# A two-layer transformer block on one core: projection in pieces within the attention plan, spectral fold at its end

## The chip, the cores and the metric

The kernel runs on one NeuronCore of one Trainium2 chip. The metric is the time of one execution in microseconds on the device, lower is better. The engines are named as in the profile: PE (TensorE, matmuls), PEld (its weight loads), DVE (VectorE), ACT (ScalarE), POOL (GpSimd) and SP (SyncE, which here issues nearly all DMAs).

## What is computed

```python
def proj(w):                                    # L0 attention: 16 heads of 16, 2 batches x 2048 tokens x 256
    return (x @ w).reshape(b, l, N_HEADS, HEAD_DIM).transpose(0, 2, 1, 3)
q, k, v = (proj(q_w), proj(k_w), proj(v_w))
scores = jnp.einsum('bhid,bhjd->bhij', q, k) / scale + alibi[None]
scores = jnp.where(causal[None, None], scores, -jnp.inf)
out = jnp.einsum('bhij,bhjd->bhid', softmax(scores), v) ... @ o_w
...
y = jnp.real(ifft(einsum('bnd,do->bno', fft(x), w)))     # L0 feed-forward: spectral, linear in x
...
x = _layernorm(x + _L0_attn_ref(...)); x = _layernorm(x + _L0_ffn_ref(...))
x = _layernorm(x + _L1_attn_ref(...)); x = _layernorm(x + _L1_ffn_ref(...))
```

The second layer (a channel attention and eight experts) is not touched by the change.

## The kernel before

The program has a front part, which computes the first attention up to its division by the softmax sums, and a back part with all the rest. Each engine walks the same list of steps (`front_plan`, then a back plan) and issues its own instructions of each step, so the list fixes the order on every engine.

**Projection.** The 4096 tokens are 8 tiles of 512; tiles 0 to 3 are batch 0. For each tile `TurnX` transposes x (L803), four `Project` steps (L820, 128x512 in f32) give two halves of q and of k, and two `Values` steps (L834) give v. ACT takes a projected half from PSUM as bf16 (L1213, the high part), DVE forms the rest (L1377), ACT its bf16 (L1216, the middle part), POOL what is left (L1749, the low part), and SP stores the three parts to `split_dram` (L1826) from one of four buffers `parts`. ACT waits for the store that last used a buffer (`parts_out`) before it writes that buffer again.

**Attention.** A unit is one batch and four of its sixteen heads: 8 units, u0 to u7. SP loads a unit's operands from `split_dram` in one of three places: 4 loads of constant key rows (L1873), one of query rows (L1878), 24 of 64 KB (L1888) and 6 of 256 KB (L1886), 35 DMAs in all. A first pass (`Chunk`, L875 with the masks of L881) computes scores into a ring of two PSUM slots of two banks, and DVE takes their row maxima (L1398). After each quarter of a unit (`Maxima`, qt 0 to 3) POOL splits the maxima, PE turns them (`SendMaxima`, L889), DVE copies them (L1414), and SP writes them as three more operand rows (L1839, `max_t`). Only then may the second pass of that quarter begin: `Score` (L909, three PSUM banks), `exp` on ACT (L1231), `Select` on POOL for the diagonal blocks (L1769), `Weigh` (L927: probabilities times v). `TakeSums` and `Divide` (L938) end a quarter. `Attention` orders these by estimated times for each engine.

**Order before.** Four tiles are projected, then come `Operands(0)`, `FoldSpectral` (L847, L854: three 256x256 products that fold the spectral weights into one matrix) and `Operands(1)`. Tiles 4 to 7 then alternate with chunks of u0, `PULL_A` columns for each piece; `Operands(2)` follows, and then the first `Score`. Projection has PSUM banks of its own (2, 3, 7, and 0 and 1 for the transposes). `x_t` holds all of x transposed.

Of the kernel before, what the change touches and what calls it, by code (L numbers as in the profile page):

```python
# [43 lines left out]
PULL_A = 1536  # L44
# [12 lines left out]
AT_A, AT_SPEC = 2 * OPS, OPS  # L57
# [5 lines left out]
PROJECT_BANKS = (2, 3, 7)  # L63
# [7 lines left out]
TurnX = namedtuple("TurnX", "tile half")  # L71
Project = namedtuple("Project", "tile side m n bank rested copied slot")
Values = namedtuple("Values", "tile half n bank rested copied")
FoldSpectral = namedtuple("FoldSpectral", "")
Operands = namedtuple("Operands", "u scored first count")
LOADS = 1 + len(TERMS) * (1 + QT)
PadRow = namedtuple("PadRow", "")
ClearSums = namedtuple("ClearSums", "")
Chunk = namedtuple("Chunk", "u qt r heads c width per_bank ring slot before")
Maxima = namedtuple("Maxima", "u qt t ring turned_before")  # L80
SendMaxima = namedtuple("SendMaxima", "u qt t ring slot before")
# [4 lines left out]
Divide = namedtuple("Divide", "u qt t ring slot before")  # L86
Residuals = namedtuple("Residuals", "ring")


class FrontPlan:  # L90


    def __init__(self):
        self.steps = []
        self.n_bank = self.n_split = self.n_values = 0
        self.bank_rested, self.bank_copied = {}, {}
        self.ring_slots, self.ring_at, self.ring_of = [0, 1], 0, {}

    def ring(self):
        n, slot = self.ring_at, self.ring_slots[self.ring_at % len(self.ring_slots)]  # L100
        before = self.ring_of.get(slot, -1) + 1
        self.ring_of[slot] = n
        self.ring_at += 1
        return n, slot, before

    def bank(self, rests):
        b = PROJECT_BANKS[self.n_bank % (2 if self.ring_at else 3)]
        self.n_bank += 1
        rested, copied = self.bank_rested.pop(b, 0), self.bank_copied.pop(b, 0)
        if rests:  # L110
            self.bank_rested[b] = self.n_split + 1
        else:
            self.bank_copied[b] = self.n_values + 1
        return b, rested, copied

    def project_tile(self, tile):
        self.steps += [TurnX(tile, 0), TurnX(tile, 1)]
        for side in range(2):
# [39 lines left out]

STRIPE = 32
UNIT_COLUMNS = GH * LENGTH * (LENGTH + P) // 2 // P  # L160


class Attention:

# [161 lines left out]
    def step(self):  # L326
# [21 lines left out]
        if self.act < self.pe + 1400:  # L348
            order.append("score")
# [1744 lines left out]
```

## Time and profile before

| | us |
|---|---|
| median of 3 runs (lowest, highest) | 1605.79 (1602.51, 1612.28) |
| profiled execution | 1608.99 |
| span of its trace | 1607.2 |
| PE, DVE, ACT, POOL busy in it | 1425.7, 1069.6, 862.0, 240.7 |

The profiled execution took 1.8 us more than the span of its trace and 3.2 us more than the median. Busy time of PE counts an instruction from start to its modelled end, so overlapping matmuls hide gaps that their starting times show.

### The profile page before, as it was taken

What the parts mean: (1) busy time and instruction counts of PE and PEld (TensorE: products, weight loads), DVE (VectorE), ACT (ScalarE), POOL (GpSimd) and SP (SyncE); (2) the same over time, 40 slices, a digit from 0 to 9 for tenths busy, and PEclk for the clock granted to TensorE, in tenths of its full rate; (3) what the DMA queues carried; (4) which work ended last, traced back from release to release, by engine and by line L of the source; (5) the groups of instructions that cost most, each with busy time, mean ns of one, the idle gap of its engine ahead of it and who ended that gap; (6) DMA issues with size and microseconds to landing.
All of it is one profiled execution on the core that took longest, in us unless ns stands there. A gap on an engine that the chain in (4) does not pass through costs nothing. (4 is left out here: it accounts for less than half of the span.)

```text
span 1607.2 us, 43807 instructions
## 1 busy us (share of the span) xinstructions
PE 1425.7 (89%) x18356; PEld 856.1 (53%) x18356; DVE 1069.6 (67%) x1985; ACT 862.0 (54%) x1791; POOL 240.7 (15%) x380
## 2 busy tenths in 40 slices
PE   7657749999989999999999999899877639999998
PEld 4433314444444444444444443487754329999997
DVE  2135538888888878888888884165357736776776
ACT  3212336776767767767677677664325513333333
POOL 4212201111110111002110120000012531111111
PEclk9979969999999999999999999899798859999999
DMA  7794550131322412315120000282004154545451
GB/s 239 147 125 116 117 52 3 27 45 21 52 28 35 62 21 37 42 30 68 20 48 3 3 4 2 77 297 64 1 0 160 57 195 161 190 168 189 169 191 71
DMA packets 76383, 134.08 MB, mean 83 GB/s; under 512 B 11938, under 2 KB 62619, under 8 KB 70812
## 3 DMA queue, kind: packets, MB, share of 16 engines
q1 hardware_dynamic: 69612, 120.14, 31.0%
q0 software_dynamic: 3408, 8.43, 1.5%
q8 instruction: 146, 2.39, 0.7%
q10 hardware_dynamic: 3168, 2.72, 0.6%
q14 instruction: 49, 0.40, 0.1%
HBM read 67.77 MB, written 23.11 MB: 57 GB/s over the span
## 5 line engine op out<-in xcount | busy, mean ns | idle before, releaser
L1398 DVE TENSOR_REDUCE part_max<-pair 128x2 f32<-128x1024 f32 (+2 forms) x576 | 645.0, 1162 | 144.8 <-PE pair L881 85.1
L1231 ACT ACTIVATE big<-pair 128x512 f32<-128x512 f32 (+1 forms) x1120 | 566.7, 613 | 233.0 <-PE pair L909 230.6
L875 PE MATMUL pair<-big 128*32 128x512 bf16 (+3 forms) x5120 | 357.4, 350 | 39.5 <-DMA big<-split_dram 24.9
L909 PE MATMUL pair<-big 128*32 128x512 bf16 (+3 forms) x5120 | 354.9, 352 | 36.3 <-DMA big<-max_t 34.1
L927 PE MATMUL pair<-big 128*17 128x512 f32 (+3 forms) x2560 | 281.8, 529 | 12.6 <-POOL big L1769 7.9
L875 PEld LDWEIGHTS pair<-big 128*32 128x32 bf16 x5120 | 136.0, 97 | 201.3 <-DVE part_max L1398 71.4
L909 PEld LDWEIGHTS pair<-big 128*32 128x32 bf16 x5120 | 126.4, 96 | 208.8 <-ACT big L1231 104.6
L1244 ACT ACTIVATE std<-moments,eps_col 128x1 f32<-128x1 f32 (+1 forms) x110 | 32.5, 295 | 258.4 <-DVE moments L1441 258.4
L1769 POOL TENSOR_SCALAR_AFFINE_SELECT big<-big 128x512 f32<-128x512 f32 x128 | 80.0, 635 | 513.7 <-ACT big L1231 513.7
L1145 PE MATMUL pair<-big,tok 128*128 128x128 f32 x1248 | 147.7, 277 | 2.7 <-DMA tok<-big 1.5
L1145 PEld LDWEIGHTS pair<-big,tok 128*128 128x128 f32 x1248 | 147.2, 194 | 5.2 <-DVE big L1669 3.3
L1157 PE MATMUL pair<-big 128*128 x624 | 141.0, 379 | 0.0
L1157 PEld LDWEIGHTS pair<-big 128*128 128x128 f32 x624 | 115.6, 190 | 14.1
L927 PEld LDWEIGHTS pair<-big 128*17 128x17 f32 x2560 | 68.5, 96 | 75.9 <-issue 35.6
L881 PE MATMUL pair<-masks,ident_b 128*32 128x128 bf16 x2048 | 101.5, 221 | 0.0
L1806 POOL DMA_INDIRECT out<-big x39 | 38.4, 984 | 262.6 <-DVE big L1710 262.6
L820 PE MATMUL pair<-big 128*128 128x512 f32 x128 | 65.1, 649 | 8.5 <-issue 5.2
L881 PEld LDWEIGHTS pair<-masks,ident_b 128*32 128x32 bf16 x2048 | 56.5, 98 | 25.3 <-issue 18.3
L983 PE MATMUL pair<-big 128*128 128x256 f32 x256 | 58.5, 382 | 0.0
L1377 DVE SCALAR_TENSOR_TENSOR big<-pair,big 128x512 f32<-128x512 f32 x32 | 22.1, 691 | 53.8 <-ACT big L1213 53.7
L1749 POOL TENSOR_TENSOR big<-big 128x512 bf16<-128x512 f32 x32 | 37.0, 1156 | 128.9 <-ACT big L1216 128.9
L1340 ACT ACTIVATE big<-pair,columns 128x128 f32<-128x128 f32 x156 | 44.2, 365 | 20.4 <-PE pair L1145 13.9
(162 smaller groups left out, 1273.1 us busy)
## 6 DMA issues: line engine op xcount, KB each, us to landing
tok<-big SPq DMA_DIRECT2D x39, 1024.0 KB
big<-in_L_ffn_w SPq DMA_DIRECT2D x16, 1024.0 KB, 12.1
split_dram<-big SPq DMA_DIRECT2D x32, 384.0 KB, 2.7
big<-split_dram SPq DMA_DIRECT2D x192, 64.0 KB, 6.3
big<-split_dram SPq DMA_DIRECT2D x48, 256.0 KB, 7.8
big<-routed_dram SPq DMA_DIRECT2D x39, 129.0 KB, 2.1
tok<-in_L_attn_x SPq DMA_DIRECT2D x8, 512.0 KB, 11.5
big<-in_c_query_rows SPq DMA_DIRECT2D x8, 512.0 KB, 5.3
```

The costliest lines, as they stand in the source:

```text
L820: mm = pe.matmul(m.bank[step.bank], m.w_qkv0[step.side][:, c, step.m * P:(step.m + 1) * P], m.x_t[:, c, cols], start=(c == 0), stop=(c == ...
L875: mm = pe.matmul(bank[q:q + STRIPE, o:o + w], m.q_op[slot][:, step.qt, h, step.r * P + q:step.r * P + q + STRIPE], m.k_op[slot][:, h, step ...
L881: mm = pe.matmul(bank[q:q + STRIPE, o + w - P:o + w], m.ident_b[:, q:q + STRIPE], m.masks[:, 1, :], start=False, stop=True, skip_group_che ...
L909: mm = pe.matmul(m.bank[step.bank][k:k + STRIPE, n * w:(n + 1) * w], m.k_op[slot][:, h, step.kb * P + k:step.kb * P + k + STRIPE], m.q_op[ ...
L927: mm = pe.matmul(m.sums[32 * h:32 * h + HD + 1, q0:TILE], m.v_aug[:, b * BPB + kb, g * GH + h, :], m.p_ring[:, place, h, at:at + TILE - q0 ...
L983: mm = pe.matmul(m.bank[b][:, j * D:(j + 1) * D], m.turned_x[slot][:, c, r * P:(r + 1) * P], weight[:, c, :], start=(c == 0), stop=(c == K ...
L1145: mm = pe.matmul(m.bank[b][:, j * P:(j + 1) * P], w1[:, c, f * P:(f + 1) * P], m.xln_t[i % 2][:, c, :], start=(c == 0), stop=(c == KC - 1))
L1157: mm = pe.matmul(m.bank[b][:, 0:D], m.hidden_t[i % 2][:, f, :], m.w2[:, bass.ds(e, 1), f, :].rearrange("p a n -> p (a n)"), start=(f == 0) ...
L1231: act.activation(m.p_ring[:, step.place, step.heads[0]:step.heads[-1] + 1, step.at:step.at + w], m.bank[step.bank][:, 0:len(step.heads) * ...
L1340: done = act.activation(m.hidden_t[i % 2][:, j, :], m.bank[b][:, j * P:(j + 1) * P], ACTF.Relu, bias=col[:, j, bass.ds(e, 1)])
L1398: dve.tensor_reduce(m.part_max[(step.u * QT + step.qt) % 2][:, step.r, step.heads[0]:step.heads[0] + n, step.c], banks[:, :, 0:w], X, ALU. ...
L1769: pool.affine_select(weights, weights, pattern=[[0, GH], [1, P]], compare_op=ALU.is_ge, fill=zero, base=0, channel_multiplier=-1).then_inc ...
```

## The change

The projection becomes 32 pieces: for each tile the transposes, a pair (q and k of one half), the values, and the other pair. Each piece takes a slot of the first pass's ring (`take_room`), so banks 0 to 2 belong to the second pass from the beginning. One planner orders all: tiles 0 to 3 are due at once, the pieces of tiles 4 to 7 when the second pass has done set shares of a unit. ACT's two copies of a projected half are separate steps, `High` and `Middle`. There are three `parts` buffers instead of four. For u0 operands are loaded tile by tile (`FirstOperands`: 12 loads of 64 KB when a tile's first pair is stored), the constant rows of u0 ahead of them. The copies of v are shared by ACT and DVE. The spectral fold and its five loads stand behind the last unit's first pass, in the ring. The planner's constants change a little (LAG 70 to 80, PE_LAG 170 to 190, ROWS_LAG 2500 to 3000, and the costs of some steps), and two blocks are weighed together only when both are ready.

```diff
-PULL_A = 1536
+PARTS = 3
...
+def project_pieces():
+    for tile in range(TILES):
+        yield "turn", tile, 0
+        yield "project", tile, 0
+        yield "values", tile, 0
+        yield "project", tile, 1
...
+    def project_due(self):
+        late = self.n_project - 4 * TPB
+        return late < 0 or self.score_columns > UNIT_COLUMNS * (0.1 + late / (4 * TPB))
 
...
-        unit = self.chunks[self.n_chunk][0]
-        now = self.scores[min(self.n_score, len(self.scores) - 1)][0]
-        done = self.score_columns / len(UNITS)
-        if self.n_score and (unit > now + 1 or self.max_columns > self.score_columns + self.lead()):
+        u, qt = self.chunks[self.n_chunk][:2]
+        at = self.operands_at.get((u, qt))
+        lead = UNIT_COLUMNS * (1 - 0.5 * self.score_columns / (len(UNITS) * UNIT_COLUMNS))
+        if at is None or self.max_columns > self.score_columns + lead:
             return None
-        return self.ring_at()
...
+    def project(self):
+        kind, tile, m = self.projects[self.n_project]
+        self.n_project += 1
+        if kind == "turn":
+            room = self.take_room("turn", tile)
+            self.steps.append(TurnX(tile, room))
+            self.pe += 900
+            self.act = max(self.act, self.pe + self.PE_LAG) + 500
+            self.dve = max(self.dve, self.pe + self.PE_LAG) + 620
+            self.free[room.slot] = self.turned_at[tile] = max(self.act, self.dve) + self.LAG
+        elif kind == "values":
+            room = self.take_room("values", tile)
+            self.steps.append(Values(tile, room))
+            self.pe += 3450
+            self.act = max(self.act, self.pe + self.PE_LAG) + 500
+            self.dve = max(self.dve, self.pe + self.PE_LAG) + 620
+            self.free[room.slot] = self.valued_at[tile] = max(self.act, self.dve) + self.LAG
+        else:
+            room = self.take_room("pair", self.n_pair)
+            self.steps.append(Project(tile, m, self.n_pair, room))
+            for side in range(2):
+                n = 2 * self.n_pair + side
+                self.pe += 1720
+                self.flush_middles(False)
+                self.steps.append(High(tile, side, m, n, n % PARTS))
+                self.act = max(self.act, self.pe + self.PE_LAG) + 500
+                self.dve = max(self.dve, self.act + self.LAG) + 620
+                self.middles.append((Middle(tile, side, m, n, n % PARTS), self.dve + self.LAG))
+            self.free[room.slot] = self.dve + self.LAG
+            self.n_pair += 1
+    def flush_middles(self, force):
+        while self.middles and (force or self.middles[0][1] <= self.act):
+            step, at = self.middles.pop(0)
+            self.steps.append(step)
+            self.act = max(self.act, at) + 520
+            self.pool = max(self.pool, self.act + self.LAG) + 1160
+            if step.side == 1:
+                self.stored(step)
+    def stored(self, step):
+        at = self.pool + 12000
+        if step.tile < TPB and step.m == 0:
+            self.steps.append(FirstOperands(step.tile, step.n))
+            self.operands_at[0, step.tile] = at
+        if (step.tile, step.m) == (TPB - 1, 0):
+            self.steps.append(Operands(1, 0, step.n, 0, LOADS))
+            for qt in range(QT):
+                self.operands_at[1, qt] = at + 28000
+        if (step.tile, step.m) == (TILES - 1, 1):
+            self.steps.append(Operands(2, 0, step.n, 0, LOADS))
+            for qt in range(QT):
+                self.operands_at[2, qt] = at + 28000
 
...
+    def fold(self):
+        n, room = self.take_ring()
+        if self.folds.pop(0) == "first":
+            self.fold_ring = n
+            self.steps.append(FoldFirst(n, room))
+            self.pe += 7100
+            self.dve = max(self.dve, self.pe + self.PE_LAG) + 1250
+        else:
+            self.steps.append(FoldSecond(n, self.fold_ring, room))
+            self.pe += 3600
+            self.dve = max(self.dve, self.pe + self.PE_LAG) + 1100
+        self.free[room.slot] = self.fold_at = self.dve + self.LAG
...
 def front_plan():
     plan = FrontPlan()
-    steps = plan.steps
-    for tile in range(TPB):
-        take(plan.project_tile(tile), 6)
-    steps += [Operands(0, 0, 0, LOADS), FoldSpectral(), Operands(1, 0, 0, LOADS)]
-    attention = Attention(plan)
-    owed = 0
-    attention.chunk()
-    for tile in range(TPB, TILES):
-        for _ in plan.project_tile(tile):
-            owed += PULL_A
-            while attention.max_columns < min(owed, UNIT_COLUMNS):
-                if attention.to_send and attention.to_send[0][-1] <= attention.pe:
-                    attention.send()
-                attention.chunk()
-    steps += [PadRow(), Operands(2, 0, 0, LOADS), ClearSums()]
-    while attention.step():
+    while plan.step():
         pass
-    plan.divided_ring = attention.divided_ring
+    plan.ring_at = plan.n_ring
+    assert not plan.loads and not plan.folds and plan.n_project == len(plan.projects)
     return plan
 
 
...
+def wait_room(pe, s, room):
+    if room.taken:
+        pe.wait_ge(s.ring_taken, room.taken)
+    if room.turned:
+        pe.wait_ge(s.xt_by_act, room.turned)
+        pe.wait_ge(s.xt_by_dve, room.turned)
+    if room.rested:
+        pe.wait_ge(s.rested, room.rested)
+    if room.valued:
+        pe.wait_ge(s.v_by_act, room.valued)
+        pe.wait_ge(s.v_by_dve, room.valued)
...
+        elif isinstance(step, Project):
+            pe.wait_ge(s.xt_by_act, step.tile + 1)
+            pe.wait_ge(s.xt_by_dve, step.tile + 1)
+            wait_room(pe, s, step.room)
+            for side, b in enumerate(MAX_BANKS[step.room.slot]):
+                if step.pair == 0:
+                    pe.wait_ge(s.w0_in[side], 16)
                 for c in range(KC):
...
+            if step.n >= PARTS:
+                act.wait_ge(s.parts_out[step.slot], 16 * (step.n // PARTS))
+            act.activation(m.parts[step.slot][:, 0, :], pair_bank(m, plan, step.n), ACTF.Copy,
                            scale=float(scale)).then_inc(s.high, 1)
+        elif isinstance(step, Middle):
             act.wait_ge(s.rested, step.n + 1)
             act.activation(m.parts[step.slot][:, 1, :], m.rest[step.slot][:, :], ACTF.Copy).then_inc(s.middle, 1)
 
...
+                 t["c_query_rows"].bitcast(BF16)[:, 0, :, :, :]).then_inc(s.first_in[0], 16)
     for step in plan.steps:
-        if isinstance(step, Project):
+        if isinstance(step, Middle):
             sp.wait_ge(s.low, step.n + 1)
             sp.dma_start(m.split_dram[step.side, :, step.m * P:(step.m + 1) * P, step.tile * TILE:(step.tile + 1) * TILE]
                          .rearrange("a p n -> p a n"), m.parts[step.slot][:, :, :]).then_inc(s.parts_out[step.slot], 16)
...
+            if step.n == 0:
+                sp.wait_ge(s.pool_set, 2)
+                sp.dma_start(m.routed_dram[EXPERTS * REGION:, :], m.pad_row).then_inc(s.pad_row_out, 16)
+        elif isinstance(step, FirstOperands):
+            first_operands(sp, m, s, step)
 
         elif isinstance(step, Operands):
             load_operands(sp, m, s, step)
+        elif isinstance(step, FoldLoads):
+            sp.wait_ge(s.scored, step.scored)
+            for dst, src in (("cos", "c_cos"), ("sin", "c_sin"), ("nsin", "c_nsin"), ("wr", "L0_ffn_w_freq_real"),
+                             ("wi", "L0_ffn_w_freq_imag")):
...
+def wait_parts(sp, s, n):
+    for slot in range(PARTS):
+        stored = (n - slot) // PARTS + 1
+        if stored > 0:
+            sp.wait_ge(s.parts_out[slot], 16 * stored)
...
+def first_operands(sp, m, s, step):
+    wait_parts(sp, s, step.stored)
+    cols = slice(step.tile * TILE, (step.tile + 1) * TILE)
+    for i in range(len(TERMS)):
+        rows = slice(EXTRA + i * HD, EXTRA + (i + 1) * HD)
+        sp.dma_start(m.k_op[0][rows, :, cols], operand_source(m, 0, i, 1, cols)).then_inc(s.first_in[step.tile], 16)
+        sp.dma_start(m.q_op[0][rows, step.tile, :, :], operand_source(m, 0, i, 0, cols)).then_inc(s.first_in[step.tile], 16)
...
-                for i in range(4):
```

In the order of instructions this shows at three places. (`pair0` to `pair3` are PSUM banks 0-1, 2-3, 4-5, 6-7; an instruction's first shape is what its rows multiply.)

SP, from the last loads of `Operands(1)` (L1888, L1886) to the first maxima rows (L1839). Before, with L1826 a store of parts:

```order
L1888 DMA big<-split_dram 16x4x512 x4
L1886 DMA big<-split_dram 16x4x2048
L1826 DMA split_dram<-big 128x3x512 x8
L1839 DMA big<-max_t0 1x16x128 x3
L1826 DMA split_dram<-big 128x3x512 x8
L1831 DMA routed_dram<-big 128x258
L1873 DMA big<-in_c_key_rows 32x2048 x4
```

The same engine in the changed kernel, where L2015 and L2013 are the last of `Operands(1)`, L1927 a store and L1948 maxima rows:

```order
L2015 DMA big<-split_dram 16x4x512 x4
L2013 DMA big<-split_dram 16x4x2048
L1927 DMA split_dram<-big 128x3x512 x2
L1948 DMA big<-max_t0 1x16x128 x3
L1948 DMA big<-max_t1 1x16x128 x3
L1927 DMA split_dram<-big 128x3x512 x2
```

The first maxima rows stood eight stores behind `Operands(1)`, and the ones of the next quarter behind `Operands(2)`; now the first ones stand two stores behind `Operands(1)`, and the two quarters' rows follow each other.

ACT, the first tile. Before, each high part (L1213) has its middle part (L1216) right behind it:

```order
L1206 ACTIVATE big<-pair 128x2x256
L1213 ACTIVATE big<-pair 128x512
L1216 ACTIVATE big<-big 128x512
L1213 ACTIVATE big<-pair 128x512
L1216 ACTIVATE big<-big 128x512
```

In the changed kernel (L1299 x transposed, L1306 high, L1317 v, L1311 middle):

```order
L1299 ACTIVATE big<-pair2 128x2x256
L1306 ACTIVATE big<-pair3 128x512 x2
L1317 ACTIVATE big<-pair2 128x32x16
L1311 ACTIVATE big<-big 128x512 x2
L1306 ACTIVATE big<-pair3 128x512 x2
L1299 ACTIVATE big<-pair2 128x2x256
```

The middle parts now stand behind the copy of v, and so do the store and all that waits for it.

PE, the end of the last unit's first pass. Before (L889 turns the last maxima, L927 weighs, L909 scores, L938 divides):

```order
L909 MATMUL pair<-big 32x128 x16
L927 MATMUL pair<-big 17x384 x4
L889 MATMUL pair<-ident_b,max_parts 48x128
L927 MATMUL pair<-big 17x256 x4
L927 MATMUL pair<-big 17x128 x4
L909 MATMUL pair<-big 32x512 x4
```

In the changed kernel (L932 and L943 the fold, L978 the maxima):

```order
L1014 MATMUL pair<-big 17x384 x4
L932 MATMUL pair<-big 128x256 x16
L978 MATMUL pair<-ident_b,max_parts 48x128
L1014 MATMUL pair<-big 17x256 x4
L1014 MATMUL pair<-big 17x128 x4
L943 MATMUL pair<-big 128x256 x8
L992 MATMUL pair<-big 32x512 x24
```

The fold's first part stands ahead of the turned maxima, its second part between them and the last quarter's scores.

## Rows read from the trace of the kernel before

**Rows 1.** Stretches: length, busy of PE, PEld, DVE, ACT, POOL; clock, DMA share, GB/s.

```profile
59.00:95.50 36.50, 10.80 (x48) 8.86 (x48) 2.57 (x5) 0.00 (x0) 0.00 (x0) 0.70 1.08 139
95.50:203.00 107.50, 85.82 (x834) 41.33 (x834) 60.29 (x68) 32.45 (x56) 23.46 (x32) 0.91 0.67 118
203.00:222.00 19.00, 0.24 (x4) 0.14 (x8) 0.00 (x0) 0.00 (x0) 0.00 (x0) 0.50 0.94 95
222.00:985.00 763.00, 738.97 (x13865) 331.70 (x13861) 626.79 (x650) 543.13 (x1075) 96.02 (x229) 0.99 0.20 29
```

**Rows 2.** PE's groups by shape, 300 to 900 us: count, then busy us and mean ns.

```profile
L909 PE MATMUL pair<-big 128*32 128x512 bf16 x2600 | 209.3, 383 | 6.4 <-DMA big<-max_t 6.4
L875 PE MATMUL pair<-big 128*32 128x512 bf16 x2624 | 204.3, 380 | 4.7 <-DVE part_max L1398 3.1 <-issue 1.5
```

**Rows 3.** Timeline of PE (start us, us, what): the second tile, then the long stretch.

```profile
21.20 1.04 PE L803 MATMUL pair<-ident,tok 128*128 128x128 f32 x8
...
23.07 7.10 PE L820 MATMUL pair<-big 128*128 128x512 f32 x16 [0.83 <-ACT big L1206]
...
33.47 1.04 PE L803 MATMUL pair<-ident,tok 128*128 128x128 f32 x8
...
304.57 0.39 PE L909 MATMUL pair<-big 128*32 128x512 bf16 x4
304.79 1.03 PE L927 MATMUL pair<-big 128*17 128x512 f32 x8
305.64 0.60 PE L875 MATMUL pair<-big 128*32 128x512 bf16 x8
```

**Rows 4.** Timeline of POOL in the first tile and ACT in the second.

```profile
16.73 1.15 POOL L1749 TENSOR_TENSOR big<-big 128x512 bf16<-128x512 f32 x1 [0.71 <-ACT big L1216]
...
25.06 0.60 ACT L1213 ACTIVATE big<-pair 128x512 bf16<-128x512 f32 x1 [2.58 <-PE pair L820]
...
26.41 0.63 ACT L1216 ACTIVATE big<-big 128x512 bf16<-128x512 f32 x1 [0.76 <-DVE big L1377]
```

**Rows 5.** The DMAs of L1826, the stores of parts.

```profile
DMA to landing us min/median/max: 2.6/2.7/24.0
```

**Rows 6.** Timeline of SP's DMA issues around the first two batches of loads.

```profile
59.21 1.77 SPq L1873 DMA_DIRECT2D big<-in_c_key_rows  x4
...
61.48 1.83 SPq L1888 DMA_DIRECT2D big<-split_dram  x4
...
185.60 1.77 SPq L1873 DMA_DIRECT2D big<-in_c_key_rows  x4
```

**Rows 7.** Timeline of PE: the matmuls that those batches hold up.

```profile
95.53 0.30 PE L875 MATMUL pair<-big 128*32 128x128 bf16 x4 [24.94 <-DMA big<-split_dram]
...
221.76 1.04 PE L909 MATMUL pair<-big 128*32 128x512 bf16 x8 [25.60 <-DMA big<-max_t]
```

**Rows 8.** DMA issues from 180 to 230 us: KB each, median us to landing.

```profile
big<-split_dram SPq DMA_DIRECT2D x24, 64.0 KB, 12.6
big<-split_dram SPq DMA_DIRECT2D x6, 256.0 KB, 13.8
...
big<-max_t SPq DMA_DIRECT2D x5, 4.0 KB, 16.5
```

**Rows 9.** DVE's commonest reduction, 300 to 900 us: count, busy us, mean ns.

```profile
L1398 DVE TENSOR_REDUCE part_max<-pair 128x2 f32<-128x1024 f32 x327 | 386.8, 1221 | 50.4 <-PE pair L875 37.8 <-PE pair L881 10.3
```

**Rows 10.** Timeline of PE at the fold.

```profile
58.93 7.14 PE L847 MATMUL pair<-big 128*128 128x256 f32 x32 [0.78 <-ACT big L1223]
...
66.86 3.72 PE L854 MATMUL pair<-big 128*128 128x256 f32 x16 [0.79 <-DVE big L1383]
```

**Rows 11.** Timeline: ACT after the last unit's first pass, PE's first work behind the front.

```profile
987.20 0.60 ACT L1231 ACTIVATE big<-pair 128x512 f32<-128x512 f32 x1 [0.21 <-PE pair L909]
...
992.64 0.60 ACT L1231 ACTIVATE big<-pair 128x512 f32<-128x512 f32 x1 [1.46 <-PE pair L909]
...
1026.30 3.56 PE L961 MATMUL pair<-ident,tok 128*128 128x128 f32 x16 [0.81 <-DVE tok L1430]
```

More of the change, by code:

```diff
@@ L61 @@
 EARLY = (AT_X - W_BYTES) * EXPERTS // W_BYTES
-PROJECT_BANKS = (2, 3, 7)
 SCORE_BANKS, SUMS_BANK, MAX_BANKS = (0, 1, 2), 3, ((4, 5), (6, 7))
 TURN_BANKS, PRODUCT_BANKS, ROUTE_BANK, FOLD_BANKS = (0, 1), (2, 3, 4), 5, (6, 7)
[L71 to L75, printed above, removed]
+Room = namedtuple("Room", "slot taken turned rested valued")
+TurnX = namedtuple("TurnX", "tile room")
+Project = namedtuple("Project", "tile m pair room")
+High = namedtuple("High", "tile side m n slot")
+Middle = namedtuple("Middle", "tile side m n slot")
+Values = namedtuple("Values", "tile room")
+FoldLoads = namedtuple("FoldLoads", "scored")
+FoldFirst = namedtuple("FoldFirst", "ring room")
+FoldSecond = namedtuple("FoldSecond", "ring first room")
 LOADS = 1 + len(TERMS) * (1 + QT)
-PadRow = namedtuple("PadRow", "")
-ClearSums = namedtuple("ClearSums", "")
-Chunk = namedtuple("Chunk", "u qt r heads c width per_bank ring slot before")
+FirstOperands = namedtuple("FirstOperands", "tile stored")
+Operands = namedtuple("Operands", "u scored stored first count")
+Chunk = namedtuple("Chunk", "u qt r heads c width per_bank ring room")
 Maxima = namedtuple("Maxima", "u qt t ring turned_before")
-SendMaxima = namedtuple("SendMaxima", "u qt t ring slot before")
+SendMaxima = namedtuple("SendMaxima", "u qt t ring room")
 Score = namedtuple("Score", "u qt kb q0 heads n bank before ring_clear first place at")
@@ L138, in max_pieces @@
             if 2 * left <= TILE:
[L139 removed]
+                pieces.append((tuple(range(GH)), qt, left, 4 if r == 0 else 2))
             else:
@@ L335, in step, with end_first_pass @@
+    def end_first_pass(self):
+        slot = self.slots[(self.n_room + 1) % 2]
+        self.slots = [1 - slot]
+        for bank in MAX_BANKS[slot]:
+            self.banks.insert(0, bank)
+            self.ring_clear[bank] = self.last_in[slot][1] + 1
+            self.bank_at[bank] = -1
+        self.exped_at[-1] = self.free[slot]
+    def step(self):
+        if self.n_chunk == len(self.chunks) and not self.to_send and len(self.slots) == 2:
+            self.end_first_pass()
         ready = {name: at for name, at in (("send", self.send_at()), ("divide", self.divide_at()), ("chunk", self.chunk_at()),
-                                           ("score", self.score_at()), ("weigh", self.weigh_at())) if at is not None}
+                                           ("score", self.score_at()), ("weigh", self.weigh_at()),
+                                           ("project", self.project_at()), ("fold", self.fold_due())) if at is not None}
@@ L836, in tensor_front @@
-            mm.then_inc(s.v_projected, 1)
-        elif isinstance(step, FoldSpectral):
+            wait_room(pe, s, step.room)
+            for half, b in enumerate(MAX_BANKS[step.room.slot]):
+                for j in range(2):
+                    o = (half * 2 + j) * P
+                    for c in range(KC):
+                        mm = pe.matmul(m.bank[b][:, j * D:(j + 1) * D], m.x_t[step.tile % 2][:, c, o:o + P],
+                                       m.w_qkv0[2][:, c, :], start=(c == 0), stop=(c == KC - 1))
+                mm.then_inc(s.v_projected, 1)
+        elif isinstance(step, FoldFirst):
@@ L1989, in program @@
     front, back = front_plan(), back_plan()
+    front.pair_rooms = [step.room.slot for step in front.steps if isinstance(step, Project)]
     back.front_ring = front.ring_at
```

409 lines of the change are left out of this document (192 added, 217 removed).

## Prediction

> **What bounds the kernel now.** I read the busy time by stretch first [rows 1], then the timeline at the stretches' edges. The front part ends at about 1025 us [rows 11]; the back part, some 582 us long, is left alone. Within the front the reader is to see two kinds of time. From 222 to 985 PE is busy 739.0 of 763 us. Before that it is not: from 59 to 95.5 us it works 10.8 us, from 203 to 222 us 0.2 us, and from 95.5 to 203 us the projection of tiles 4 to 7 and most of u0's first pass share 107.5 us.
>
> The two stalls have one cause. A unit's operands are 35 DMAs. From their first issue to the matmul that waits for the last of them it is 59.21 to 95.53 us, and from 185.60 to 221.76 us for the next batch [rows 6, 7]: 36 us both times. The second time PE doesn't wait for operands but for a few KB of maxima rows that SP issued behind them: 4 KB took 16.5 us to land [rows 8].
>
> For the long stretch I need a rate. Counted by groups, 300 to 900 us held 2600 of 3584 and 2624 of 3584 full-width matmuls of the second and first pass (448 of each per unit), so a unit costs 600 x 448 / 2612 = 102.9 us [rows 2]. In PE's own pace four such matmuls take 0.213 us (304.57 to 304.79), the eight of a block's weighing 0.85 (304.79 to 305.64), and a 512-wide product of L820 as much (8 of them, which the trace counts as 16, in 6.8) [rows 3]. At this pace the first pass is 32.4 us of a unit, the second 29, weighing 29 and the rest 1.7: an estimate of 92.1 us of paced work, 0.895 of the time. As a check: from 222 us, 8 x 92.1 less 19 already done is 718 us, and 718/0.895 = 802, which ends at 1024, as the trace does.
>
> PE's busy share says 97% there, my pace 89.5%. The Trainium skill (Perfetto Trace Analysis, Identifying the Most-Contended Engine) warns that matmul busy time is no measure of closeness to the roofline, since matmuls are pipelined. By the busy share, moved work would cost 3% more than its pace, by mine 12%; over 45 us that is 4 us.
>
> **Part 1: tiles 0 to 3.** Before, a tile starts every 12.3 us (21.20 to 33.47) [rows 3]. Pieces in the ring cost PE the same 11.1 us. What is new is a circle through SP. A `High` must wait for the store three halves earlier, and from now on that store stands in SP's queue behind `FirstOperands`, which waits for the landing of the tile's first pair and then issues 12 loads. The circle: High 0.6, copy of v 0.6, two middles 1.26, low 1.15 [rows 4], store landing 2.7 [rows 5], 12 loads at 0.46 = 5.5 (1.83 for four) [rows 6], the next store's landing 2.7: 14.5, with two issues of stores and the hand-overs about 16 us a tile instead of 12.3. PE waits the difference. The first `FirstOperands` can start at about 23.4 us (before, the second low part ends at 17.88 [rows 4]; its middle now stands behind the copy of v, some 2.4 us later, and the store adds 3.1), the fourth at 71.4, and its loads are issued by 77.
>
> **Part 2: the first scores.** `Operands(1)` follows at once on SP, and the first maxima rows behind it. Nothing between differs from the two batches that took 36 us, so the first score starts at 77 + 36 = 113 us, not at 222. Meanwhile PE has only 13 chunks (6 us paced) and idles from about 85 us. So of two stalls one stays, about 28 us long. The rule that fits is in the Trainium skill (DMA: Bandwidth & Descriptors, Queues, rings and completion order): an engine consumes the descriptors of one queue in ring order. The trace agrees by 16.5 us for 4 KB [rows 8]; without such an order the first score could start at about 85.
>
> **Part 3: what is left at 113 us.** Attention 8 x 92.1 - 6 = 731, and four tiles x 11.1 = 44.4: 775 us, at 0.895 866 us. Before, the same account ran 802 us from 222. That gives 979 for the end of the front.
> Corrections: (a) a piece of the projection runs 3.4 us without a hand-over, so its 44 us cost about 46, not 50: -3.6. (b) The lead of the first pass must be built. Before, 222 us found most of u0's maxima done; now the order has runs of 7 to 10 chunks with no score between quarters of u0. Each costs DVE 1.22 us [rows 9] and PE 0.43, about 0.75 us of PE idle: some 17 chunks above what the order before has, +13. (c) ACT and ring waits around the eight pairs of tiles 4 to 7, some close together with three `parts` buffers: between 0 and 10, I take +3, nearest to ACT's 0.6 us a copy, one for every second piece [rows 4].
> (d) The fold. Before, its 7.14 and 3.72 us lay under the first load stall and cost nothing [rows 10]. Now they stand where PE turns the last maxima. ACT's gap there was 987.8 to 992.6 us [rows 11]; `FoldFirst` delays the turn by 7 us, `FoldSecond` lies under the 3 us flight of the rows: +8.5. Bounds: 5 (ACT still has work) and 11 (all of it). Its loads move from the first 6 us to u5 and lie under PE.
> (e) The planner's new constants change the long stretch little: between -8 and +8, I take 0; the order there differs in single places.
>
> Sum: 979 - 3.6 + 13 + 3 + 8.5 = 1000, against 1025: 25 us less. From the profiled execution, 1609.0 - 25 = 1584. This execution stood 3 us above the median of 1605.79; the forecast is 1584 for the median as well, within what such a difference means.
>
> **Rivals.**
> More gain. The projection pieces may fill what PE loses in attention: of the 102.9 us of a unit 10.8 are no paced work, and 44 us of moved projection lie over 1.4 units. If the score rate holds while they run, up to 15 us of them are free; and if the lead costs nothing (13), the time is 1556. If the loads run sooner because u0's are spread over the projection, it is also there. For it: DVE and ACT have slack (627 and 543 of 763 us). Against: PE holds both, and a piece starves both for 3.4 us.
>
> The loads by number. `FirstOperands` fetches keys in 24 loads of 64 KB instead of 6 of 256 KB. Landings were 12.6 and 13.8 us for the two sizes, hardly different [rows 8]; if a load's place in the queue costs the same whatever its size, 36/35 = 1.03 us each, a tile's 12 loads take 12.3 us in place of 5.5, the circle 23 us, the first score starts at 23.4 + 3 x 23 + 5.5 + 36 = 134, and the time is 1605: nothing gained. The Trainium skill (Perfetto Trace Analysis, DMA Optimizations) speaks for this rival: larger DMAs use the bandwidth better, and transfers under 2 KB carry much overhead. The runs of the key loads fall from 4 KB to 1 KB. By that rule the time would be near 1605, by the rate of the two batches 1584; the landings of rows 8 leave both open.
>
> Slower: ACT blocks in order. With `High` and `Middle` in one queue with the exponentials, each pair holds one ring slot until DVE's rest, which may queue behind two reductions (2 x 1.22), and ACT stands still until then. At 6 us for each of the 8 pairs and 1.5 for each transposing and value piece (60 us) the time is 1641. The time passes that of before when the pairs together cost 25 us more than forecast, 3 us each. Against it: the planner places `Middle` behind further scores.
>
> The change doesn't do what it says: projection of tiles 4 to 7 isn't spread, since all its pieces lie within u0's scores and the first of u1. Then part of (b) and (c) grows: within the second and third case.
>
> **How the numbers follow.** Forecast (1573 to 1600) 0.45; more gain (1545 to 1573) 0.27; loads by number (1600 to 1620) 0.20; slower 0.08. The range 1552 to 1612 leaves out about a tenth on either side and takes in the bounds of (b) to (e). A measurement here tells about 1%, 16 us, from no change. Below 1589.7 lie all of the second case and 0.33 of the first: 0.6; above 1621.9 the last: 0.07; the rest is the same.
>
> **What the profile after would show.** The first score at 105 to 122 us, waiting for maxima rows, and one stall of PE ahead of it with the lower clock; tiles 0 to 3 starting 16 us apart, with ACT waiting for a store; runs of reductions on DVE with PE waiting for them in u0; the front's end near 1000; ACT idle for 13 us around the fold. The prediction is wrong if the first score starts near 85 or 135 us, or if a unit after the third takes other than 102.9 us.

## The result, and the profile after

The changed kernel takes 1618.17 us (median of 5 runs, 1616.91 to 1623.38), the kernel before 1606.81 beside it (1602.51 to 1612.28). The ratio is 1.0074, with a 95% interval of 1.0046 to 1.0103: 0.7% slower, where I forecast 1584. The profiled execution has a span of 1616.9 us.

The timeline of PE in the changed kernel, at the two places where it stands longest, and at the front's end:

```profile
86.99 0.62 PE L965 MATMUL pair<-big 128*32 128x512 bf16 x8 [0.29 <-DVE part_max L1501]
119.45 1.47 PE L992 MATMUL pair<-big 128*32 128x512 bf16 x12 [31.84 <-DMA big<-max_t]
...
317.81 0.22 PE L978 MATMUL pair<-ident_b,max_parts 128*48 128x128 bf16 x1
...
321.64 0.41 PE L1014 MATMUL pair<-big 128*17 128x128 f32 x8
351.16 1.47 PE L992 MATMUL pair<-big 128*32 128x512 bf16 x12 [29.11 <-DMA big<-max_t]
...
1037.14 1.09 PE L1047 MATMUL pair<-ident,tok 128*128 128x128 f32 x8 [0.81 <-DVE tok L1528]
```

Before, PE had the stalls of [rows 7], 24.94 and 25.60 us, and reached the back part at 1026.30 [rows 11]. The matmul at 221.76 us that the prediction calls the first score is that of u0's second quarter. The first quarter's scores are a little work done ahead of the stall:

```profile
185.35 0.83 PE L909 MATMUL pair<-big 128*32 128x512 bf16 x12 [0.34 <-ACT big L1223]
```

So the first score now starts 66 us sooner (119.45 against 185.35). But again there are two stalls, 31.84 and 29.11 us, both ended by rows of maxima; the front ends 10.8 us later. What SP does ahead of them, in its timeline (the line at 99.91 is the first of three rows):

```profile
81.74 1.75 SPq L1966 DMA_DIRECT2D big<-in_c_key_rows  x4
...
98.90 0.96 SPq L1927 DMA_DIRECT2D split_dram<-big  x2
99.91 3.71 SPq L1948 DMA_DIRECT2D big<-max_t  x1
...
307.25 1.75 SPq L1966 DMA_DIRECT2D big<-in_c_key_rows  x4
...
328.20 1.35 SPq L2015 DMA_DIRECT2D big<-split_dram  x3
329.59 2.62 SPq L1948 DMA_DIRECT2D big<-max_t  x3
```

The second stall is `Operands(2)`, 35 loads from 307.25, in among which u3's single loads stand. PE turned u1's third quarter of maxima at 317.81; SP issued the rows at 329.59, 11.8 us later, and PE got them at 351.16, another 21.6. The first is made alike: turned at 83.40, issued at 99.91, in PE at 119.45, 19.5 us after that. The stretches (span, then busy us and count for PE, PEld, DVE, ACT, POOL; granted clock, DMA share, GB/s):

```profile
80.00:99.90 19.90, 4.25 (x105) 1.74 (x97) 8.53 (x10) 0.00 (x0) 0.83 (x4) 0.75 1.01 146
99.90:119.40 19.50, 0.00 (x0) 0.00 (x0) 0.00 (x0) 0.00 (x0) 0.00 (x0) 0.50 0.98 128
307.00:329.60 22.60, 15.01 (x260) 6.46 (x258) 13.32 (x15) 10.71 (x22) 3.32 (x8) 0.91 1.03 134
329.60:351.10 21.50, 0.00 (x0) 0.00 (x0) 0.00 (x0) 0.00 (x0) 0.00 (x0) 0.50 1.11 115
```

In all four the 16 DMA engines are full (share 0.98 to 1.11) at 115 to 146 GB/s, and in the two stalls the granted clock is the lower level, 1.2 GHz. The tiles' starts and the fold, in the timelines of PE and then ACT:

```profile
22.45 1.04 PE L897 MATMUL pair<-ident,tok 128*128 128x128 f32 x8
40.41 1.04 PE L897 MATMUL pair<-ident,tok 128*128 128x128 f32 x8
59.90 1.04 PE L897 MATMUL pair<-ident,tok 128*128 128x128 f32 x8
...
992.23 7.17 PE L932 MATMUL pair<-big 128*128 128x256 f32 x32
...
1000.95 3.69 PE L943 MATMUL pair<-big 128*128 128x256 f32 x16 [0.61 <-DVE max_t L1517]
```

```profile
990.93 1.08 ACT L1323 ACTIVATE big<-pair 128x512 f32<-128x512 f32 x2 [0.87 <-PE pair L992]
1000.41 0.60 ACT L1331 ACTIVATE acc_t<-pair 128x512 f32<-128x512 f32 x1 [8.39 <-PE pair L1014]
1005.02 1.58 ACT L1323 ACTIVATE big<-pair 128x512 f32<-128x512 f32 x3 [4.02 <-PE pair L992]
```

### The profile page after: what moved, and what is told of

It is laid out like the page before. It is cut to its first block and busy times, and to the rows that moved or that the text cites. A ratio compares the mean times of both kernels' runs of the same rounds, so it can differ in the third digit from the quotient of the medians.

```text
span 1616.9 us, 43840 instructions
## 1 busy us (share of the span) xinstructions
PE 1421.3 (88%) x18356; PEld 858.1 (53%) x18356; DVE 1075.9 (67%) x1993; ACT 854.5 (53%) x1783; POOL 240.4 (15%) x380
## 5 line engine op out<-in xcount | busy, mean ns | idle before, releaser
L965 PE MATMUL pair<-big 128*32 128x512 bf16 (+3 forms) x5120 | 362.3, 354 | 28.3 <-DVE part_max L1501 23.4
L1243 PEld LDWEIGHTS pair<-big 128*128 128x128 f32 x624 | 115.6, 190 | 14.1
L1432 ACT ACTIVATE big<-pair,columns 128x128 f32<-128x128 f32 x156 | 44.3, 365 | 19.5 <-PE pair L1231 11.3
L1069 PEld LDWEIGHTS pair<-big 128*128 128x128 f32 x256 | 50.3, 200 | 7.0
```

Source lines behind the costliest of these rows:

```text
L965: mm = pe.matmul(bank[q:q + STRIPE, o:o + w], m.q_op[slot][:, step.qt, h, step.r * P + q:step.r * P + q + STRIPE], m.k_op[slot][:, h, step ...
L1069: mm = pe.matmul(m.bank[b][:, j * D:(j + 1) * D], m.turned_x[slot][:, c, r * P:(r + 1) * P], weight[:, c, :], start=(c == 0), stop=(c == K ...
L1243: mm = pe.matmul(m.bank[b][:, 0:D], m.hidden_t[i % 2][:, f, :], m.w2[:, bass.ds(e, 1), f, :].rearrange("p a n -> p (a n)"), start=(f == 0) ...
L1432: done = act.activation(m.hidden_t[i % 2][:, j, :], m.bank[b][:, j * P:(j + 1) * P], ACTF.Relu, bias=col[:, j, bass.ds(e, 1)])
```

## The experiments

Each of the three groups of runs (1 to 4, 5 to 8, 9 to 12) has its own runs of the kernel before beside it (medians 1606.66, 1607.71 and 1599.98 us). So that they can be compared I give each run as its ratio to before with the 95% interval, and the ratio times 1606.8 us; the changed kernel is 1618.7 in this count. "Less" is against the changed kernel.

**1. Rows of maxima by ScalarE's queue** (changed kernel).

```diff
+        elif isinstance(step, SendMaxima) and step.t < ROWS_BY_ACT:
+            act.wait_ge(s.ring_taken, step.ring + 1)
+            for a, row in enumerate(MAX_ROWS):
+                act.dma_start(m.q_op[step.u % 3][row:row + 1, step.qt, :, :].rearrange("o h n -> o (h n)"),
...
-        elif isinstance(step, SendMaxima):
+        elif isinstance(step, SendMaxima) and step.t >= ROWS_BY_ACT:
```

> The changed kernel, with one edit: the rows of maxima of the first eight quarters are issued by ScalarE's queue and not by SyncE's. Theory (the rows land late because they stand behind operand loads on SyncE's queue): both long waits of TensorE for max_t go, the 31.8 us ahead of the first score and the 29.1 us at 322 to 351; the first score starts near 90 instead of 119.45, and the time falls by 45 to 60 us, to 1558 to 1573. Rival (the 16 DMA engines are taken by the loads, whichever queue the rows come from): the rows take as long to land, both waits stay within 3 us, and the time stays within 6 us of 1618. Second rival (ScalarE's own order): one of the two waits only changes its place, and the time falls by 25 to 30 us.

0.994 (0.9925 to 0.9955), 1597: 21 us less, where I expected 45 to 60. The stalls shrank to 7.59 and 11.16 us, so 42 us of waiting went; half of it came back elsewhere. 11.4 us are two stops of PE for which the trace shows no releaser ("issue"; last section), and ACT waits more. ACT's waits from 60 to 350 us:

```profile
ACT big L1324 <- PE pair L993: 77.9, 50, 18.6
...
ACT acc_t L1338 <- issue: 15.1, 1, 15.1
ACT acc_t L1338 <- DVE part_max L1508: 13.4, 1, 13.4
ACT acc_t L1338 <- PE pair L972: 9.0, 1, 9.0
```

L1338 is the copy of a quarter's sums. In the changed kernel it waits 6.9 us in 4 times from 100 to 400 us, each time for its own weighing. Now it stands behind ACT's wait for the next quarter's maxima: 37.5 us in three times, with the exponentials queued behind it. Not all of this is ACT's order: PE stood from 107.28 to 112.30 us (5.02) in the middle of the chunk whose maxima the 15.1 us waited for. Landing itself: at 303.20 the rows went out from ACT's queue and still took 14.6 us (median, against 18.9 from SP's), with the loads running.

**2. The same edit in the kernel before.**

> The kernel before, with the same one edit: the rows of maxima of the first eight quarters by ScalarE's queue. Theory of the queue's order: the wait at 203 to 222 (25.60 us for max_t) shrinks to under 6 us and the time falls by 19 to 25 us against the kernel before, to 1582 to 1588. Rival of the taken DMA engines: within 6 us of the kernel before. If the queue's order is all that stands between the two kernels, this kernel and the one of the first run keep the distance that the lead and the fold give.

0.9991 (0.9978 to 1.0004): nothing. The stall at 222 falls from 25.60 to 11.86 us, and the front's end only from 1026.3 to 1023.6. The rival's time came, but not for its reason alone, since the stall did shrink. ACT issued the rows at 194.01, where SP had issued them at 203.87: 10 us are SP's own list. From issue to PE it was 14.2 instead of 17.9 us. Of the 13.7 us won, PE's waits for ACT took 5 back (5.2 us from 60 to 350, 0.3 before) and one stop without a releaser 3.35; the rest isn't traced.

**3 and 4. Loads one by one among the scores.** Unit 2's alone, then those of units 1 and 2, each after every second score; the rows stay with SP.

```diff
-            self.steps.append(Operands(2, 0, step.n, 0, LOADS))
+            self.loads = [Operands(2, 0, step.n, n, 1) for n in range(LOADS)] + self.loads
...
-            self.steps.append(Operands(1, 0, step.n, 0, LOADS))
+            self.loads = [Operands(1, 0, step.n, n, 1) for n in range(LOADS)]
...
-        if self.loads and n % 4 == 0:
-            self.steps.append(self.loads.pop(0))
+        if self.loads and n % {1: 2, 2: 2, 3: 3}.get(self.loads[0].u, 4) == 0:
```

> The changed kernel, with the 12 operand loads of unit 2 issued one at a time, one after every second score of unit 0, instead of in one row while unit 1's maxima are made; the rows of maxima stay on SyncE's queue. Theory: only the second long wait (29.1 us at 322 to 351) goes, the first (31.8 us) stays; 26 to 31 us less than the changed kernel, near 1589. Rival of a DMA engine bound: the transfer is merely earlier, when the engines have room, so this rival expects the same here and is told apart by the first run alone. Rival of ScalarE's order: within 6 us of 1618.

> As the run before, and unit 1's 12 operand loads one at a time too, one after every second score of unit 0. Theory: both long waits go, the first score starts near 90, and the time is 52 to 61 us under the changed kernel, 1557 to 1566. Rival (the loads among the scores hold up SyncE's other work, so that units 1's scores start late): a new wait of TensorE at the change from unit 0 to unit 1 takes 10 to 30 us of it back, 1570 to 1595.

(There are 31 load steps a unit, not the 12 that the expectations speak of; the edit is the one shown.) Unit 2 alone: 0.9944 (0.9917 to 0.9971), 1598, 21 us less, short of the 26 to 31 expected; the first stall stays (30.58), the second becomes 5.90. Both: 0.975 (0.9719 to 0.9781), 1567, 52 us less, the lower end of what I expected. PE in the fourth run:

```profile
86.75 0.83 PE L992 MATMUL pair<-big 128*32 128x512 bf16 x12 [0.43 <-DMA big<-max_t]
...
294.15 1.47 PE L992 MATMUL pair<-big 128*32 128x512 bf16 x12 [7.23 <-DMA big<-max_t]
...
303.29 0.59 PE L965 MATMUL pair<-big 128*32 128x512 bf16 x5
309.90 0.61 PE L965 MATMUL pair<-big 128*32 128x512 bf16 x3 [6.02 <-issue]
```

The first score starts at 86.75, 33 us sooner, and its wait is gone. The 7.23 us at 294 are left because unit 2's loads wait for its projection, stored at about 270, and then run in a row again.

**5. The fold back in front**, behind u0's first `SendMaxima`, its constants loaded at the start.

> The changed kernel, with the spectral fold put back to the front, right behind the first quarter's maxima, its five constants loaded at the start by ScalarE's queue. Theory: the fold costs its time at the end of the front only because nothing else is left for TensorE there; under the first long wait for max_t it is free, and the gap of about 13 us between the two fold products at 992 to 1005 goes back to about 5. 6 to 11 us less than the changed kernel, 1607 to 1612. Rival: it lengthens the row of work ahead of the first score instead, and the time stays within 3 us of 1618.

1.0063 (1.0039 to 1.0087), 1617: the rival was right, no difference that can be told. From the last quarter of u6 to that of u7 it is 87.8 us (952.47 to 1040.26 in L1025), against 93.0 in the changed kernel: 5.2 us come back. In front the fold lay under the stall as meant (PE L933 at 87.32, L944 at 95.94, then 25.16 us of waiting), and yet the rows were issued 4.2 us later (104.08), the first score came at 124.79, and u1 ended 6.7 us later (444.04). The third tile already started at 44.07 instead of 40.41: in the first 30 us the DMA engines were 0.95 busy in place of 0.85, with the fold's five constants among the first stores. What moved work costs can lie with its loads.

**6. Four buffers of parts.**

```diff
-PARTS = 3
+PARTS = 4
...
+            if step.n >= 3:
+                dve.wait_ge(s.low, step.n - 2)
```

(The buffers of the rest stay three, which is what the added wait is for.)

> The changed kernel, with four buffers for the three-part operands of the projection instead of three (the buffers of the rest stay three). Theory (the circle of parts, stores and loads through SyncE's queue sets a tile's pitch of 16 to 19.5 us): the pitch falls to about 13, the first score starts 8 to 14 us earlier than 119.45, and the time falls as much, 1604 to 1610. Rival (the store's own landing or TensorE sets the pitch): pitch as before, the time within 3 us of 1618.

1.0006 (0.9987 to 1.0026), 1608: 11 us less, as expected. ACT's waits from 0 to 90 us, first of the changed kernel:

```profile
ACT big L1306 <- DMA split_dram<-big: 22.5, 6, 6.4
```

and with four buffers:

```profile
ACT big L1306 <- DMA split_dram<-big: 7.3, 4, 3.3
```

Tiles start at 22.51, 35.13 and 48.55 us, 12.6 and 13.4 apart instead of 18.0 and 19.5; the first score at 107.97. Both long stalls stay (32.38 and 29.78), so this gain is one of its own.

**7 and 8. Combinations**: parts, fold in front, and either the loads one by one (7) or the rows by ScalarE's queue (8).

> The changed kernel with three edits in one: four buffers of parts, the fold in front, and the loads of units 1 and 2 one by one. Theory, as a sum of the terms: 29 + 30 + 8 + 10 us less than 1618, near 1541 (1530 to 1560). Rival (the terms overlap: with the first wait gone the fold in front has no cover and the parts' circle no slack): 1560 to 1575.

> The changed kernel with four buffers of parts, the fold in front, and the rows of maxima of the first eight quarters by ScalarE's queue, the loads in rows as they are. Theory of the queue's order: near 1545 (1532 to 1562), as the run before. Rival of the taken DMA engines: the two long waits stay and only the parts and the fold count, near 1600.

0.9754 (0.972 to 0.9788), 1567, as the rival had it and no better than the fourth run, and 0.9905 (0.9876 to 0.9935), 1592, near its rival's 1600. The front of the seventh ended at 988.3 us, 2.9 sooner than the fourth's, and its back part was 5 us longer. So parts and fold together gave next to nothing on top of the loads. The eighth looks like runs 1 and 12: ACT's copy of the sums waited 33.0 us in two times, and PE had two stops of 7.39 and 7.16 us without a releaser. It does not tell the two apart.

**9. Parts and loads, the fold at the end.**

> The changed kernel with four buffers of parts and the loads of units 1 and 2 one by one; the fold stays at the end. Theory (the two terms stand in different places and add, and it was the fold in front that cost the seventh run its gain): 50 + 11 us less than the changed kernel's 1618, 1552 to 1562. Rival (the parts' 11 us are lost once the first score follows its rows at once, since VectorE or the projection is then late): 1565 to 1573, as the fourth and the seventh run.

0.9704 (0.9649 to 0.9758), 1559: 60 us less than the changed kernel. The terms of runs 4 and 6 (52 and 11) add. The front ends at 977.1 us, 11.3 sooner than in run 7, whose only difference is the fold in front. But the two belong to different groups, and the back part, the same program in both, was 10 us shorter too (574.8 against 585.1); the ratios are 8 us apart with intervals that overlap. What the fold's place is worth here is not shown.

**10. The projection's last pieces due sooner.**

```diff
-        return late < 0 or self.score_columns > UNIT_COLUMNS * (0.1 + late / (4 * TPB))
+        return late < 0 or self.score_columns > UNIT_COLUMNS * (0.1 + late / (6 * TPB))
```

> As the run before, and the projection's later pieces fall due sooner (its 16 last pieces over two thirds of a unit's scores instead of a whole one), so that unit 2's operands can be loaded some 20 us earlier. Theory (in the fourth run 7.2 us at 294 and 6.0 us at 310 are waits behind unit 2's loads, which cannot start before its projection is stored): both waits fall under 1 us, 8 to 13 us less than the ninth run. Rival (those waits come with the loads wherever they stand, as the 16 DMA engines are full for 30 us): within 4 us of the ninth run.

0.9664 (0.963 to 0.9697), 1553: 3.4% less than before, the fastest of all. The gain over run 9 is about 6 us (front's end 971.6 against 977.1), less than the 8 to 13 expected; the intervals overlap. Three edits separate this run from the changed kernel: the loads, the fourth buffer and the due times. What PE waited for rows from 60 to 1045 us is 62.0 us in the changed kernel

```profile
PE pair L992 <- DMA big<-max_t: 62.0, 4, 31.8
```

and in this one 2.4 us, in four waits; the front's longest wait is 3.04 us at 301.44, once more a stop without a releaser.

**11. The planner told.** It takes a quarter's rows as landed 20 us after they are sent, not 3, for the first eight quarters.

```diff
-        self.sent_at[u, qt] = self.dve + self.ROWS_LAG
+        self.sent_at[u, qt] = self.dve + (self.ROWS_LAG if t >= 8 else 20000)
```

> The changed kernel, with one number of the planner's: for the first eight quarters it takes the rows of maxima as landed 20 us after they are sent, not 3 us. Nothing else moves but what the plan then chooses. Theory (behind a row of loads the rows land 15 to 19 us after their issue; the planner did not know, so it left projection and maxima undone that could fill the time): some of the 60.9 us of waiting is filled by chunks and projection; it falls to 25 to 40 us, and the time to 1590 to 1610. Rival (nothing that is free to run is left at these places, because maxima and projection wait for the same loads): within 5 us of 1618, or slower, since the lead of the first pass is spent.

0.9894 (0.9857 to 0.993), 1590: 29 us less, by one number, the lower end of what I expected. The loads stand in rows as they did. PE's long waits:

```profile
119.09 1.47 PE L992 MATMUL pair<-big 128*32 128x512 bf16 x12 [14.38 <-DMA big<-max_t]
...
330.62 3.62 PE L1014 MATMUL pair<-big 128*17 128x512 f32 x16 [7.76 <-issue]
345.04 0.61 PE L992 MATMUL pair<-big 128*32 128x512 bf16 x8 [3.74 <-issue]
```

The first score starts no sooner, but PE has worked meanwhile, up to 104.7 us, on u0's later chunks. The second wait for rows is gone; the two lines behind it are stops without a releaser.

**12. Run 10 with the rows by ScalarE's queue.**

> As the tenth run, and the rows of maxima of the first eight quarters issued by ScalarE's queue. Theory: with the loads one by one the order of SyncE's queue costs nothing more, so this is within 4 us of the tenth run. Rival (SyncE's queue still holds rows back behind loads): 4 to 10 us less.

0.9824 (0.9788 to 0.9859), 1579: 26 us more than run 10. Both the theory and its rival miss. ACT at the first of its long waits:

```profile
84.69 0.60 ACT L1324 ACTIVATE big<-pair 128x512 f32<-128x512 f32 x1 [0.67 <-PE pair L993]
98.57 1.81 ACTq L1331 DMA_DIRECT2D big<-max_t  x3
100.43 0.60 ACT L1338 ACTIVATE acc_t<-pair 128x512 f32<-128x512 f32 x1 [15.14 <-issue]
```

ACT issues the rows at 98.57, and until then nothing: no chunk's work is ACT's, but the sums and the next scores queue behind. Three such waits make 37.1 us from 60 to 350 us. But PE in the same time:

```profile
90.64 0.39 PE L966 MATMUL pair<-big 128*32 128x512 bf16 x1 [0.87 <-DVE part_max L1510]
96.11 1.04 PE L966 MATMUL pair<-big 128*32 128x512 bf16 x7 [5.08 <-issue]
```

PE had begun the chunk whose maxima the rows need and stood 5.08 us in the middle of it, where its list has nothing to wait for. PE's waits of this kind from 60 to 350 us are

```profile
PE pair L966 <- issue: 17.4, 3, 6.9
PE pair L1015 <- issue: 4.8, 1, 4.8
```

22.2 us, and 6.3 in run 10. That is 16 of the 26 us. Waits for rows are 5.5 us longer than in run 10 and waits for ACT 3.4. So ACT's place in the order costs something, as in runs 1 and 2, but it doesn't explain the loss alone, and why PE stops more often in this run is open.

## Why the prediction was wrong

**The failed step** is in part 2: "So of two stalls one stays, about 28 us long." I looked for the stall at `Operands(1)` only. `Operands(2)` has no term in the sum and no reason is given for that; I took its stall as gone with the old order. But it is still 35 loads in one row, and the changed plan puts u1's third quarter of maxima in the middle of them, with a planner that believes rows to land in 3 us. That stall is 29.11 us. Run 3 takes most of it away (5.90 left) and wins 21 us, run 11 fills it. With it the forecast would have been 1584 + 29 = 1613, no difference from before.

**Part 1, the circle through SP**: right in kind and nearly in size. On PE the tiles start 15.9, 18.0 and 19.5 us apart, against 16, but the four `FirstOperands` on SP, which set the first score, start so:

```profile
26.27 0.35 SPq L1989 DMA_DIRECT2D big<-split_dram  x1
42.08 0.34 SPq L1989 DMA_DIRECT2D big<-split_dram  x1
58.85 0.34 SPq L1989 DMA_DIRECT2D big<-split_dram  x1
75.56 0.35 SPq L1989 DMA_DIRECT2D big<-split_dram  x1
```

They are 15.8, 16.8 and 16.7 us apart. The fourth is 4.2 us late against 71.4: 2.9 come from the first (26.27, forecast 23.4) and 1.3 from three rounds of the circle. `Operands(1)` starts at 81.74 instead of 77. Run 6 shows that the three buffers are the cause of the pitch.

**Part 2, the batch**: 81.74 to 119.45 is 37.7 us, against 36. The first score was forecast for 113; the 6.5 us are part 1's 4.7 and this 1.7. "Not at 222" compared it with the second quarter's: the 64 matmuls of the first quarter's scores and their weighing were done by then, and the 19 us of paced work "already done" leave them out, which by the prediction's paces is about 4 us. But the reason that I gave, ring order, is only a part. SP issues the rows 16 us after it could have, as it works off its own list; after that the rows land late mostly because the engines are full, since from the other queue it is 14.6 instead of 18.9 us (run 1), and 2.5 us in run 4, where the first rows go out among single loads. The Trainium skill says so (DMA: Bandwidth & Descriptors, Issuing engines are not separate DMA queues): DMAs of all issuers interleave on the same 16 engines. The trace agrees by these landings. I had cited the Trainium skill's rule on ring order and not this one.

**Part 3, the rate**: a unit after the third takes 101.1 us. The last divisions (L1024) of u1 and u6 stand at 437.36 and 942.73 us. Grouped by form, PE did between them:

```profile
L992 PE MATMUL pair<-big 128*32 128x512 bf16 x2240 | 177.0, 383 | 1.8 <-DMA big<-max_t 1.1 <-issue 0.3
L965 PE MATMUL pair<-big 128*32 128x512 bf16 x2240 | 173.9, 381 | 4.4 <-DVE part_max L1501 4.2
```

That is 5 x 448 of each in 505.4 us. The prediction set 102.9 as its own test, and this is 1.8 us a unit off: 9 us in the kernel's favour, which I had not forecast. The kernel before gives 103.2 when counted so (422.57 to 938.71).

**(b), the lead**: reductions with PE waiting stand where forecast, 13.0 us in 25 waits from 100 to 400 us, as the 13 forecast (before, 1.0 us in 2 from 222 to 400). Yet from the first score to u1's end (437.36), without the second stall, it is 288.8 us, where the forecast's own terms leave 277.9 (1000 - 94.6 for the last unit with the fold - 5 x 102.9 = 390.9, less 113). The granted clock behind the two stalls may be some of it:

```profile
119.40:140.00 20.60, 16.83 (x277) 7.41 (x277) 14.99 (x16) 6.39 (x13) 3.37 (x8) 0.75 0.01 3
...
351.10:370.00 18.90, 18.67 (x292) 8.28 (x292) 12.75 (x13) 12.70 (x24) 0.00 (x0) 0.86 0.42 45
```

The shortfall here is 20.6 x 0.25 + 18.9 x 0.14 = 7.8 us of full clock. The kernel before has such a stretch too, behind its stall at 222, and the forecast's rate was taken with it: 0.87 over 222.0 to 242.6 us, 2.7 us. So at most 5.1 of the 10.9 us come from these stretches. (It is a little low elsewhere too, 0.94 over 150 to 180 and 0.89 over 385 to 400 us, while PE waits for reductions.) No run shows the clock's part alone, and the rest stays open.

**(d), the fold**: the last unit takes 93.0 us (942.73 to 1035.68), 86.1 before (938.71 to 1024.83): +6.8, and 5.2 by run 5, against 8.5 (5 to 11). ACT's gap is 13.0 us (992.01 to 1005.02, but for one copy) as forecast. By run 5 the fold's place is no loss against the front in this order: what it costs at the end comes back at the start.

The sum, in the forecast's count: 1000 + 6.5 (first score) + 29.1 (second stall) + 10.9 (u0 and u1) - 9.1 (u2 to u6) - 1.6 (last unit) = 1035.8; the trace has 1035.68. It must close, since the terms are the differences of one timeline; it shows where the time lies and not why. The second stall is 29 of the 36 us; the other four misses, +17 and -11, leave 7. That they nearly cancel is luck. The back part is unchanged (579.8 us from 1037.14, 580.9 before).

**The rivals.** The measured time lies in the range of "the loads by number", but that was not it: a tile's 12 small loads were issued in 5.5 us (58.85 to 64.35) and held nobody for 12.3, and its first score at 134 did not come. "Slower: ACT blocks in order" did not happen in this kernel (from 60 to 350 us ACT waited 1.0 us for DVE's rest), but something like it came in runs 1, 2 and 12, which put one more wait into ACT's list. That the loads in one row are the trouble, and not the change's structure, is shown by run 4: the same projection, ring, buffers and fold, 2.5% faster than before. What is not shown is whether the change itself gains anything, since no run gave the kernel before its loads one by one.

## What to carry to other kernels

Count the stalls by their cause, not by their place: every row of loads that the new order still holds will stall what is issued behind it, wherever the new plan puts it. A planner's latency for a DMA must be what it is behind the planner's own loads; one number for it was worth 29 us here, and feeding the loads in one by one 52. Before giving a small DMA to another engine's queue, ask what that engine has to wait for before it may issue it, and who stands behind: of the four runs that did it (1, 2, 8 and 12) none was faster by as much as its waits for rows shrank.

## What was not expected of the hardware

PE stops where no semaphore is waited for, mostly in the middle of a group of eight matmuls: in the fourth run 5 are done at 303.29 and 3 at 309.90, after 6.02 us of "issue". Stops over 4 us stand in runs 1 (5.02 and 6.41), 4 (6.02), 7 (4.09), 8 (7.39 and 7.16), 11 (7.76) and 12 (5.08, 4.85, 5.42 and 6.87), all from 90 to 345 us; the kernel before and the changed kernel have none in their fronts. The DMA queues of the fourth run from 306 to 309 us (packets, MB, share of 16 engines):

```profile
q1 hardware_dynamic: 203, 0.35, 105.4%
q8 instruction: 1, 0.02, 3.2%
```

There are such instruction packets all through the program (146 in the changed kernel) that hold nobody. In each of the eleven stops named exactly one moves; in the shorter ones of run 10 (2.61 and 3.04 us) none does. That the fetch of PE's next instructions is late behind the loads fits them, but one packet in some 11 us is the mean anyway, and no run was made for it.

Operand loads fill the engines at 115 to 125 GB/s (329.6 to 351.1 and 97 to 120 us): of the 2457 packets from 97 to 120 us 2198 are under 2 KB. From 80 to 90 us in the fourth run, mostly stores and constant rows with the same engines at a share of 0.79, it was 211 GB/s.

The clock stayed low behind a stall too: 0.75 granted over the 20.6 us behind the first (PE busy 16.83 us), 0.86 over the 18.9 us behind the second (18.67). Before it was 0.87 over the 20.6 us behind the stall at 222 (PE busy 20.49).
